# An audio tower on one core: expert attention with row-tiled scores, block maxima two units ahead and keys padded by masked weights

## The reference, cut to what matters

```python
sx = einsum('bsh,ndh->bnsd', x, hl_w) + hl_b       # 4 heads n of d = 16
q = einsum('bnsd,neod->bneso', sx, wq)             # 4 experts e
k = einsum('bnsd,nod->bnso', sx, wk)
v = einsum('bnsd,nod->bnso', sx, wv)
scores = einsum('bnesd,bntd->bnest', q, k) * d ** 0.5 + causal
att = softmax(scores, axis=-1)
qkv = where(pad, 0, einsum('bnest,bntd->bnesd', att, v))
gs = softmax(einsum('bnsf,nef->bnse', out, gate_w) + gate_b)
mixed = einsum('bnsed,bnse->bnsd', out, gs)
hn = layernorm(mixed + resid, ln_g, ln_b)          # then two 16x16 layers, a norm and a gate by head
```

## Time and profile before

| | before |
|---|---|
| median of 3 runs | 1997.99 us (1995.75 to 2002.71) |
| profiled execution, its own time | 2006.71 us |
| span of its profile | 2004.9 us |
| TensorE busy over the span | 1719.6 us (86%) |
| VectorE busy over the span | 1488.5 us (74%) |
| ScalarE busy over the span | 756.6 us (38%) |
| GpSimd busy over the span | 690.5 us (34%) |
| mean granted TensorE clock | 0.865 of 2.4 GHz |

### The profile page before, as it was taken

The page is one execution under the profiler, slowest core; times in us unless marked ns, Lnnn a source line. Parts: engine busy times, 40 slices in busy tenths (PEclk is TensorE's granted clock), DMA queues, the critical chain, the costliest instruction groups (busy, mean ns, idle before and its releaser), DMA issues. The chain is left out here.

```text
span 2004.9 us, 45616 instructions
## 1 busy us (share of the span) xinstructions
PE 1719.6 (86%) x15064; PEld 1344.4 (67%) x15064; DVE 1488.5 (74%) x4423; ACT 756.6 (38%) x2274; POOL 690.5 (34%) x957
## 2 busy tenths in 40 slices
PE   1499999999769999999999999973999999788887
PEld 1266666666557777777777777752888888677776
DVE  6166676666627898888889888875766665688887
ACT  2245454545324444344344444321222222343442
POOL 2622222222134555545545445532211111322221
PEclk9999999999869999999999999985555555788788
DMA  2000000000000000000000000000000000000000
GB/s 114 1 2 0 0 0 0 0 0 0 1 1 1 1 2 0 0 0 0 0 0 0 0 0 0 1 1 0 1 0 0 0 0 1 1 5 8 4 6 11
DMA packets 6980, 8.13 MB, mean 4 GB/s; under 512 B 6272, under 2 KB 6272, under 8 KB 6784
## 3 DMA queue, kind: packets, MB, share of 16 engines
q1 hardware_dynamic: 6912, 7.25, 1.1%
HBM read 5.71 MB, written 1.54 MB: 4 GB/s over the span
## 5 line engine op out<-in xcount | busy, mean ns | idle before, releaser
L1142 ACT ACTIVATE ex_pT<-ex_T 128x376 f32<-128x376 f32 (+1 forms) x384 | 162.8, 440 | 217.1 <-PE ex_T L1044 207.9
L604 ACT ACTIVATE al_prob<-al_S,al_negmax 94x94 f32<-94x94 f32 (+1 forms) x512 | 146.2, 375 | 180.0 <-DVE al_negmax L731 180.0
L1207 DVE TENSOR_REDUCE ex_negmax<-ex_R 94x2 bf16<-94x376 f32 (+1 forms) x384 | 186.8, 543 | 30.6 <-PE ex_R L1015 30.0
L1044 PE MATMUL ex_T<-ex_qm,ex_kpad 128*128 128x188 f32 x1024 | 189.7, 329 | 0.0
L505 PE MATMUL al_S<-al_kpad,al_qT 128*94 128x376 f32 x384 | 166.5, 516 | 0.0
L1044 PEld LDWEIGHTS ex_T<-ex_qm,ex_kpad 128*128 128x128 f32 x1024 | 163.0, 192 | 5.1
L944 POOL TENSOR_SCALAR_AFFINE_SELECT ex_pT<-ex_pT 128x512 f32<-128x512 f32 x128 | 84.3, 659 | 236.5 <-ACT ex_pT L1142 236.5
L682 POOL TENSOR_TENSOR al_kpad<-al_kT,al_quad_mask 128x1504 f32<-128x1504 f32 x32 | 86.2, 2692 | 186.3 <-ACTq L619 186.3
L731 DVE TENSOR_REDUCE al_negmax<-al_S 94x2 f32<-94x376 f32 (+1 forms) x192 | 99.1, 542 | 62.6 <-PE al_S L506 56.7
L1554 POOL TENSOR_TENSOR ta_kk<-ta_ext 94x320 f32<-94x320 f32 x64 | 60.4, 961 | 246.4 <-DVE ta_qkn L1734 163.0
L1027 PE MATMUL ex_R<-ex_sxT,wsb 128*128 128x188 f32 x256 | 72.3, 364 | 47.5 <-DVE ex_negmax L1207 47.5
(11 more groups left out here) (308 smaller groups left out, 4300.8 us busy)
## 6 DMA issues: line engine op xcount, KB each, us to landing
tok_xin<-x_t SPq DMA_DIRECT2D x4, 760.0 KB, 6.9
wsb<-weights SPq DMA_DIRECT2D x1, 2531.0 KB, 14.2
out<-stream SPq DMA_DIRECT2D x16, 94.0 KB
tok_par<-tok_w SPq DMA_DIRECT2D x1, 4.5 KB, 1.7
```

Of the source, the lines that this page charges most:

```text
L604: last = nc.scalar.activation(p[:, k, cols], S[0:P, k, cols], ACT.Exp, bias=negmax[g % 2][:, m:m + 1])
L1044: last = nc.tensor.matmul(T[:, k, (j % 2) * N:(j % 2 + 1) * N], kpad[par][:, j, 0:K0], qm[e % 2][:], start=True, stop=True)
L1142: nc.scalar.activation(pT[e % 2][rows, k, cols], T[rows, k, cols], ACT.Exp)\
L1207: red(dst, src, AX.X, ALU.max, negate=True).then_inc(sem["r_used"], 1)
```

## The change

- `scores`: a head's keys are taken from its own 32 partitions of `kT` with `tile_position=(32 * n, 0)`, fp32 as before; each head has its own bank of T (four banks), columns 0 to 187 for the first 128 keys and 188 to 247 for the last 60, which now stand on partitions 64 to 127 (the weights are columns 64 to 191 of `kT`, padded to 192 with zeros). Heads 0 and 1 come before heads 2 and 3, each pair with its own semaphore.
- `kpad` is gone, and so are GpSimd's two products. `kpadb` is made by four bf16 matmuls with masked weights `ewkb` in two new fills, kb01 and kb23, which ScalarE copies out.
- `max_scores`: R has two banks, one for the first 128 queries with 4x128 keys, one for the last 60 queries with two heads in each half of the partitions (column tiles of 64). It is issued two units ahead instead of one. `maxima` has two reductions, of 512 and 376 elements a partition.
- `queries` writes into a free part of T's bank 0, and ScalarE's exponential of heads 0 and 1 waits for it.
- Exponentials are two a unit (2x248 elements); `affine_select` covers 4x128 and 4x60 elements on all partitions.
- The order of fills and VectorE's order are rewritten. Constants are 34 instead of 21.
- Before units 0, 8 and 20 there are 16 bf16 matmuls of 512 columns into R, whose result is not used (`keep_busy`); FILLERS is 0.

```diff
+    NP = 192
+    QB = 64
+    PAIRED = NH // 2
+    PAIR = N + K1
+    QCOL = 256
+    WARM, WARM_AT = 16, (0, 8, 20)
+    FILLERS = 0
...
-        R = psum("R", [128, 3, 512])
-        T = psum("T", [128, 3, 512])
+        R = psum("R", [128, 2, 512])
+        T = psum("T", [128, NH, 512])
...
+        FILLS = [("xT", FRONT), ("znT", MLP), ("fg", LAST), ("sx", FRONT),
+                 ("pickA", TAIL), ("kb01", FRONT), ("kb23", FRONT), ("q01", FRONT),
+                 ("pickB", TAIL), ("fc1", MLP), ("k", FRONT),
+                 ("q23", FRONT), ("v", FRONT), ("fc2", MLP)]
...
-                    if e == 1 and valid(rf):
-                        pool.wait_ge(sem["kT_ready"], r + 1)
-                        for dst in (kpadb, kpad):
-                            nc.gpsimd.tensor_tensor(dst[1 - u][:], kT[:].unsqueeze(1).broadcast_to([128, NH, N]),
...
+            def padded_keys(which):
+                return [(X[:, i * N:(i + 1) * N], ewkb[:, n, :], sxb[:]) for i, n in enumerate(which)]
...
+            def keep_busy(n):
+
+                for _ in range(n):
+                    nc.tensor.matmul(R[:, 0, :], w_parts[:, 0, 0:128], w_parts[:, 0, 128:640], start=True, stop=True)
...
+                need(pe, sem["r_used"], 2 * u)
+                if isinstance(u, int) and u in WARM_AT:
+                    keep_busy(WARM)
+                keep_busy(FILLERS)
+                early = R[:, 0, :].rearrange("p (n s) -> p n s", n=NH)
+                nc.tensor.matmul(early, qTb[par][:, e, 0:K0], kpadb[par][:, :, 0:K0], start=True, stop=False)
+                nc.tensor.matmul(early, eye[:], maskA[:].unsqueeze(1).broadcast_to([128, NH, K0]), start=False, stop=True)\
+                    .then_inc(sem["r_full"], 1)
+                late = R[:, 1, 0:PAIRED * N].rearrange("p (j s) -> p j s", j=PAIRED)
+                for c in range(2):
+                    nc.tensor.matmul(late[QB * c:QB * c + QB], qTb[par][:, e, K0:NP], kpadb[par][:, c::2, :],
+                                     start=True, stop=False, tile_position=(0, QB * c), skip_group_check=True)
+                nc.tensor.matmul(late[:, :, K0:N], eye[:], maskB[:, 0:K1].unsqueeze(1).broadcast_to([128, PAIRED, K1]),
+                                 start=False, stop=True, skip_group_check=True).then_inc(sem["r_full"], 1)
...
+                for s in range(2):
+                    for n in heads:
+                        rows = slice(32 * n, 32 * n + 32)
+                        if s == 0:
+                            last = nc.tensor.matmul(T[:, n, 0:N], kT[par][rows, 0:K0], qm[e % 2][rows, :], start=True,
+                                                    stop=True, tile_position=(32 * n, 0), skip_group_check=True)
                         else:
...
+                            last = nc.tensor.matmul(T[:, n, N:PAIR], kT[par][rows, QB:NP], qm[e % 2][rows, K0:N],
+                                                    start=True, stop=True, tile_position=(32 * n, 0),
+                                                    skip_group_check=True)
...
                     nr, ne, npar = (ru, e + 1, par) if e < 3 else (rf, 0, odd)
-                    if valid(nr):
-                        max_scores(nr, npar, ne)
+                    fr, fe, fpar = (ru, e + 2, par) if e < 2 else (rf, e - 2, odd)
                     if valid(ru):
-                        scores(ru, par, e)
+                        first = scores(ru, par, e, (0, 1))
+                        if not valid(nr):
+                            first.then_inc(sem["tA_full"], 1)
+                        scores(ru, par, e, (2, 3)).then_inc(sem["tB_full"], 1)
...
+                        act.wait_ge(sem["tB_full"], u + 1)
+                        nc.scalar.activation(pT[e % 2][:, 2:4, :], T[:, 2:4, 0:PAIR], ACT.Exp).then_inc(sem["tB_used"], 1)
...
+                dve.wait_ge(sem["r_full"], 2 * u + 1)
+                red(negmaxA[e % 2][:, D::32], R[:, 0, :].rearrange("p (n s) -> p n s", n=NH), AX.X, ALU.max, negate=True)\
+                    .then_inc(sem["r_used"], 1)
+                dve.wait_ge(sem["r_full"], 2 * u + 2)
+                red(negmaxB[e % 2][:, 48:113:64], R[:, 1, 0:PAIRED * N].rearrange("p (j s) -> p j s", j=PAIRED), AX.X,
+                    ALU.max, negate=True).then_inc(sem["r_used"], 1)
```

More of the change, by code:

```diff
@@ L1032, in queries, with scores @@
-                last.then_inc(sem["m_full"], 1)
-            def scores(r, par, e):
+                for c in range(2):
+                    last = nc.tensor.matmul(T[:, 0, QCOL + K0:QCOL + N], negmaxB[e % 2][:, 32 - 32 * c:160 - 32 * c],
+                                            eye[:, QB * c:QB * c + K1], start=False, stop=True, skip_group_check=True)
+                return last
+            def scores(r, par, e, heads):
                 u = r * NE + e
                 if e == 0:
-                    pe.wait_ge(sem["kpad_ready"], 2 * r + 2)
+                    pe.wait_ge(sem["k_used"], r + 1)
@@ L1039, in scores @@
                 pe.wait_ge(sem["m_used"], u + 1)
[L1040 to L1049 removed]
+                if heads[0] == 0:
+                    pe.wait_ge(sem["tA_used"], u + 1)
+                else:
+                    need(pe, sem["tB_used"], u)
@@ L1232, in body @@
                         .then_inc(sem["fc2_used"], 1)
-                if valid(ru):
-                    maxima(ru, 1)
                 if valid(rz):
@@ L1286, in body @@
                     dve.sem_inc(sem["fg_used"], 1)
+                if valid(t):
+                    for h in range(HALVES):
+                        last = nc.vector.bn_stats(stats[:, h, :], stream[:, t * HALVES + h, :])
+                    last.then_inc(sem["stats_set"], 1)
+                if valid(t):
+                    dve.wait_ge(sem["stats_set"], t + 1)
+                    dve.sem_inc(sem["aggregate"], 1)
+                    for h in range(HALVES):
+                        last = nc.vector.bn_aggr(moments[:, h, :], stats[:, h, :])
+                    last.then_inc(sem["stats_ready"], 1)
+                if valid(rt):
+                    pick_heads(rt, 0, "pickA")
+                if valid2(rz):
+                    steps.settle()
+                    link(red(zmean[:], groups(z), AX.X, ALU.add))
+                    link(ts(zmean[:], zmean[:], -1.0 / D, None, ALU.mult))
+                    link(tt(groups(z), groups(z), over_components(zmean), ALU.add))
+                if valid(ru):
+                    maxima(ru, 3)
+                    mask_values(ru, 0, par)
+                if valid2(rz):
+                    link(tt(sq[:], z[:], z[:], ALU.mult))
+                    link(red(zvar[:], groups(sq), AX.X, ALU.add))
+                    ts(zvar[:], zvar[:], 1.0 / D, LN2_EPS, ALU.mult, ALU.add).then_inc(sem["zvar_ready"], 1)
+                if valid(rt):
+                    pick_heads(rt, 1, "pickB")
+                    dve.wait_ge(sem["pickB_used"], rt + 1)
+                    flat = gate[:].rearrange("p h n f -> p h (n f)")
+                    link(red(flat, glog[:].rearrange("p h e n f -> p h (n f) e"), AX.X, ALU.add))
+                    link(tt(flat, flat, over_halves("gate_b"), ALU.add))
+                    flat = gate[:].rearrange("p h n f -> p (h n) f")
+                    link(red(top[:], flat, AX.X, ALU.max))
+                    tt(flat, flat, top[:].unsqueeze(2).broadcast_to([P, HALVES * NH, NE]), ALU.subtract)\
+                        .then_inc(sem["gate_ready"], 1)
+                if valid(rf):
+                    maxima(rf, 0)
+                if valid(ru):
+                    mask_values(ru, 1, par)
                 if valid(rm):
```

337 lines of the change are left out of this document (143 added, 194 removed).

## The result

The changed kernel takes **2043.05 us** (median of 4 runs, 2042.23 to 2048.91), the kernel before 1999.89 (1995.75 to 2002.71) beside it: a ratio of 1.0224, 95% interval 1.0196 to 1.0252. It is slower by 2.2%, clear of no change (if not quite of 2%), where 5% faster was forecast, and it lies outside the range. The profiled execution took 2043.27 us with a span of 2041.3, against 2006.7 and 2004.9 before: 36.4 us more.

The account below looks back on a forecast made before the run. TensorE and VectorE together were taken to bound the expert stage. A turn falling from 24.13 to 20.3 us over 31 turns saves 118, less 13 fixed, so 105 us: 1902 profiled, 1893 us predicted; range 1835 to 1985.

Parts of the forecast that it names:

- Scores, 1.1 us a unit: TensorE's `scores` with row tiles: from 1.98 to 1.1 us a unit, saving 3.5 us a turn (bounds 0 and 5.1).
- the two overlapping cases: TensorE's `scores`: 0.7 us a unit if row tiles overlap like `weigh`'s column tiles, 1.4 if each head pair runs by itself.
- Maxima's scores, 0.75: TensorE's `max_scores`: from 0.81 to 0.75 us a unit, 0.2 us less a turn.
- the bound for changes of shape: TensorE's tiling mode changes: three more a unit cost between 0 and 1.7 us a turn, partly left to the range.
- TensorE 18.8 us a turn: TensorE's work a turn: 22.2 less 3.5 for scores, less 0.2 for `max_scores`, plus 0.3 for kb01 and kb23.
- VectorE 17.4, reductions 0.68 and 0.54, variance 0.6: VectorE's turn from 21.5 to 17.4 us: reductions save 1.6, variance 2.5 as it drops from 3101 ns to 0.6 us.
- Warm +8: The 48 unused matmuls of 512 columns before units 0, 8 and 20 add about 8 us together.
- What is late next, 1.5 us a turn: TensorE's remaining idle time a turn: sx waiting for fg's release, 1.0 us, and kb01 waiting for pickA's VectorE steps, 0.5.
- The clock, held at 1.00: TensorE's granted clock expected to stay at 1.00 over the expert stage, with a turn of 20.3 us.
- The rival that got 12%: Clock falls as TensorE idles more; a third of turns wholly at 1.2 GHz gives 25.5 us a turn, 2050 us; 12%.
- The argument against it: Against a falling clock: slow TensorE has no idle time, and at the stage's start, 85% busy, the clock soon rose.
- 31 turns alike: Expert stage: 3.8 us saved in about 31 of 32 turns, 118 us; the drain is bound by other chains.

Follow-up runs that it names:

- the version with both: Changed kernel with three last links moved earlier and six unused matmuls at each of the two long waits; 1941.48 us, 0.9686 to the kernel before.
- the first run: Changed kernel with one unused matmul of 512 columns ahead of every unit's maxima scores (FILLERS = 1); 2036.99 us, 1.0193 to the kernel before.
- full rows: Changed kernel with row tiles undone, scores contracting all 128 partitions, heads not separated; 2112.82 us, 1.0578 to the kernel before.
- the better order: Changed kernel with q23's copy ahead of `qm`, fg's release ahead of `mask_values`, `hx` at the end of the turn before; 1982.09 us, 0.9898.

## Why the prediction was wrong, step by step

- **Scores, 1.1 us a unit:** 0.70, the lower of the two overlapping cases. That alone would have made the kernel faster than forecast.
- **Maxima's scores, 0.75:** 0.87, and up to 1.04 where the next fill waits, with the late part at 0.28. It takes back 0.5 us a turn, 1.2 at most; the bound for changes of shape (1.7 a turn) covers it, but only the range had it.
- **TensorE 18.8 us a turn:** right, by errors that cancel: scores 1.6 a turn less, maxima 0.5 to 1.2 more, and the rest in no term. With the waits filled it is 464.06 / 500 x 22.16 = 20.6, less 16 unused matmuls of 256 columns (0.109 each, 256 / 376 of 0.16), 18.8; the version with both gives 18.9.
- **VectorE 17.4, reductions 0.68 and 0.54, variance 0.6:** 398.91 / 600 x 25.50 = 17.0; 0.696, 0.548 and 0.171. Right, or better.
- **Exponentials 0.58:** 0.584. `queries` no longer waits for the maxima: 0.7 us in all. **Constants +5:** VectorE's first instruction is 5.0 us later.

```profile
569.01 0.35 DVE L1307 BATCH_NORM_STATS2 ex_stats<-stream 94x6 f32<-94x64 f32 x2 [13.63 <-POOL ex_z L942]
```

- **Warm +8:** 8.3.
- **What is late next, 1.5 us a turn: the step that failed first.** Two of the three real waits weren't named. `hx` stood at the head of VectorE's next turn, 24.7 us in all, the longest of them, and the copy of q23 stood behind `qm` on ScalarE, 11.5. Only fg's release was seen. Kb01, put down at 0.5, isn't among the waits. They sum to 2.3 us, and a turn at full clock takes 21.9 (the undisturbed turns of the run with the waits filled) to 22.1 (the one full turn of the first run), not 20.3; 0.8 of it is in no term. By these alone the forecast would have been some 1893 + 31 x 1.7 = 1946, still faster.
- **The clock, held at 1.00: the step that turned the sign.** 25.5 - 22.0 = 3.5 us a turn. The rival that got 12% said that the clock falls, and its sentence "a turn is 25.5" is what came, with 2050 against 2043. That it fell was rightly feared; the number is luck. It put a third of the turns wholly at 1.2 GHz, at 36 us each, beside turns of 20.3. What came is every turn at 1.2 GHz for 10 or 14 us of its 25.5, from 22.0; and at 0.29 us for each of these a turn wholly at 1.2 GHz would be an estimated 22.0 / (1 - 0.29) = 31. (Its 1993 should also be 2006.7 - 8.7 = 1998, so its time was 2054.) The argument against it was wrong twice. "A slow TensorE has no idle time": at 1.2 GHz it still waits 0.96 us for `hx` and 0.80 for sx, as these chains belong to other engines. "It soon rose": it rose, too, within each turn, but after 10 to 14 us at the lower level and only to be lost again in the next. A clock lost once in each turn was not thought of.
- **31 turns alike:** the drain was 9.6 us longer, which had no term. 2.6 of it is its first turn, 25.9 us at clock 0.74 where it was 23.3 at 1.00. The other 7.0 is in its last three turns. In them GpSimd's root follows VectorE's mean and variance, and these come later:

```profile
1396.88 0.16 DVE L1300 TENSOR_REDUCE ex_top<-ex_X 94x2 f32<-94x8 f32 x1 [1.89 <-PE ex_X L992]
...
1399.65 2.93 POOL L971 TENSOR_TENSOR ex_zrstd<-ex_zvar,neg_half 94x16 f32<-94x16 f32 x1 [8.21 <-DVE ex_zvar L1329]
```

VectorE waits 1.89 us for fg before them, so the root starts 5.6 us after `hx`, where it was 3.2; the last drain turns take 12.0, 11.2 and 11.1 us, before 9.8, 8.8 and 8.8. That drain wasn't tried by itself.

So the cause of the longer time is shown: the clock is lost once in each turn, and filling two waits, with nothing else changed, brings it back to 0.99 and takes 82 us away. That the waits come with the shorter scores is shown too: with full rows the wait for `hx` is gone and the clock is 0.95. What is not shown is which of the three waits loses the clock by itself. The rows speak for their sum: with the links moved the waits are 2.0 instead of 2.3 us a turn and the clock is 0.88; of the falls in the change as made, half come behind the wait for q23 and half behind the one for `hx`. Filling only one of them, or q23's too, was not tried.

## What to carry to other kernels

When a change makes TensorE's part of a loop shorter, list every wait that TensorE then has and read the granted clock around each; waits of 2.3 us a turn cost another 3.5 through the clock here. Issue the last link of each chain earlier on its engine, but sum the waits again after it, for they move (2043 to 1982 us, with 2.0 of the 2.3 us left). Fill what is left with unused matmuls inside the wait (2043 to 1961 us), and don't expect much of them in the dense parts (2037, and 17 us lost with the better order). And ask of each relieved engine whether anything still waits for it: with GpSimd's two products put back, a turn was as long as without them.

## What the runs showed of the hardware that was not expected

- The clock was lost and won back within a turn of 25 us: down after waits of 0.46 and 0.19 us or after one of 1.02, then 1.2 GHz through 11 us with TensorE 93% busy, then up. The Trainium skill's *TensorE: Matmul & The Clock Gate*, "HAM oscillation — how this bites in real kernels", tells of a kernel whose waits for DMA of some 3 to 5 us between bursts drop the clock in each round. The runs agree that waits between bursts do it, 0.99 with them filled against 0.78; but no wait in the change's loop is longer than 1.4 us.
- With a dense TensorE behind the fall the full clock was back after 3.4 us, with two waits behind it after 13.7.
- Four row tiles of fp32 load and multiply side by side: 16 loads within 0.64 us, scores in 0.70 instead of 1.98.
- Two column tiles of 64 were not so good: 0.28 us for 376 columns where one matmul of 376 takes 0.16. Why was not tried.
